# One load of the first image up front, and a last stage without reset, in a selective scan followed by a spiking neuron

## What is computed

```python
x = x + ss2d(group_norm(x))                 # x: 8 images of 48 x 48 x 256, f32
x = x + lif(group_norm(x) @ W.T + b)        # one "time step" is one image

def ss2d(x):        # D = 512 channels, 16 states, L = 2304 positions
    xh, z = split(x @ W_in)
    xc = depthwise_conv_3x3(xh)
    dt, B, C = ...                          # from xc @ W_xproj; dt by softplus
    h = exp(dt * A) * h + (dtN * B) * xc    # scan over L, for each of 16 states
    y = sum(h * C) + Dskip * xc
    return (layer_norm(y) * silu(z)) @ W_out + b_out

def lif(h):         # over the images, one after the other; v = membrane
    v = v + (h_t - v) / 2
    s = (v >= 1)
    v = v * (1 - s)                         # the reset: used by the next image only
    return s                                # spikes
```

## Time and profile before

| | us |
|---|---|
| median of 3 runs | 4572.82 |
| lowest, highest | 4570.01, 4573.57 |
| profiled execution | 4570.02 |
| its span, first to last instruction | 4568.0 |
| TensorE, matmul busy | 3595.8 (79%) |
| VectorE busy | 4081.0 (89%) |
| ScalarE busy | 3338.8 (73%) |
| GpSimd busy | 4007.6 (88%) |

### The profile page before, as it was taken

How to read it: one execution, slowest core, us unless ns; L and a number is a source line. 1 busy time by engine, 2 the same in 40 slices (tenths; PEclk the granted TensorE clock), 3 DMA queues, 4 the chain that set the end, 5 groups by cost and what they waited for, 6 DMA issues and landing times.

```text
span 4568.0 us, 74518 instructions
## 1 busy us (share of the span) xinstructions
PE 3595.8 (79%) x20244; PEld 2243.1 (49%) x20244; DVE 4081.0 (89%) x4077; ACT 3338.8 (73%) x5698; POOL 4007.6 (88%) x2661
## 2 busy tenths in 40 slices
PE   4778888878887887878888787877887887788865
PEld 2444544545454554545554454445544554455543
DVE  0999999999999999998999999999999999999993
ACT  2777777777777777777777777777777777777772
POOL 1999999889998899988999889988999889999991
PEclk9899999999999989998999989999899999999977
DMA  3322322332233223322232223222322232223200
GB/s 76 114 66 85 101 61 72 106 88 72 66 100 96 77 59 99 90 77 73 79 102 70 77 71 100 80 73 73 106 83 63 78 108 88 59 82 95 79 29 21
DMA packets 189416, 364.40 MB, mean 80 GB/s; under 512 B 27416, under 2 KB 164120, under 8 KB 188960
## 3 DMA queue, kind: packets, MB, share of 16 engines
q1 hardware_dynamic: 188960, 359.12, 26.7%
HBM read 289.84 MB, written 69.21 MB: 79 GB/s over the span
## 4 chain that ended last, share of the span: by engine, by line
POOL 33%; issue 26%; PE 16%; DVE 16%; ACT 7%; DVEq 1%; POOLq 1%; DMA 1%; SPq 0%; ACTq 0%
POOL st L562 27%; DVE st L1003 11%; PE ht L1126 6%; DVE y L979 2%; PE work L1192 2%; POOL y L595 2%; PE work L1158 2%; ACT decay L704 2%; PE work L1163 1%; PE work L1153 1%; POOL xb L604 1%; POOL st L569 1%; PE work L1199 1%; DVE work L944 1%; PE work L1099 1%
## 5 line engine op out<-in xcount | busy, mean ns | idle before, releaser
L1003 DVE TENSOR_TENSOR_SCAN st<-decay,st 128x1024 f32<-128x1024 f32 (+1 forms) x1536 | 2732.4, 1779 | 167.6 <-ACT decay L704 75.1
L562 POOL TENSOR_TENSOR st<-xc,bbc 128x1536 f32<-128x1536 f32 x768 | 2652.2, 3454 | 25.1 <-DMA bbc<-brow 12.1
L704 ACT ACTIVATE decay<-dt,neg_a 128x1024 f32<-128x1024 f32 (+1 forms) x1536 | 1361.8, 900 | 513.8 <-DVE st L1003 510.9
L1126 PE MATMUL ht<-ident,st 128*128 128x128 f32 x9216 | 1372.4, 300 | 448.4 <-DVE st L1003 370.7
L1126 PEld LDWEIGHTS ht<-ident,st 128*128 128x128 f32 x9216 | 1145.5, 154 | 775.5 <-issue 439.7
L979 DVE SCALAR_TENSOR_TENSOR y<-ht,ct,y 128x512 f32<-128x512 f32 x1536 | 1121.6, 730 | 94.7 <-PE ht L1126 94.4
L595 POOL TENSOR_TENSOR y<-y,weighed 128x512 f32<-128x512 f32 x624 | 793.1, 1271 | 208.9 <-ACT weighed L733 206.3
L733 ACT ACTIVATE weighed<-ht,ct 128x512 f32<-128x512 f32 x624 | 426.6, 684 | 291.0 <-PE ht L1126 289.3
L1158 PE MATMUL work<-xn,win 128*128 128x384 f32 x768 | 340.9, 588 | 133.2 <-DVE volt L959 100.7
L1099 PE MATMUL work<-tri,conv_w 96*32 96x384 f32 x4608 | 430.0, 507 | 19.0 <-ACT xc L689 13.1
L1153 PE MATMUL work<-xn,win 128*128 128x480 f32 x768 | 356.4, 588 | 5.1 <-ACT xn L836 3.1
(11 more groups left out here) (100 smaller groups left out, 3535.9 us busy)
## 6 DMA issues: line engine op xcount, KB each, us to landing
bbc<-brow SPq DMA_DIRECT2D x192, 768.0 KB, 6.1
tri<-rows_of_xh SPq DMA_DIRECT2D x576, 200.0 KB, 3.9
rows_of_xh<-xhp SPq DMA_DIRECT2D x192, 250.0 KB, 2.6
xin<-in_x_dram SPq DMA_DIRECT2D x48, 384.0 KB, 3.3
out_dram<-ot SPq DMA_DIRECT2D x48, 384.0 KB, 4.1
brow<-xp SPq DMA_DIRECT2D x48, 24.0 KB, 1.5
win<-in_L_conv_W_in_dram SPq DMA_DIRECT2D x1, 1024.0 KB
wo<-in_L_conv_W_out_dram SPq DMA_DIRECT2D x1, 512.0 KB
```

What stands on the lines that cost most here:

```text
L562: u = g.tensor_tensor(slot, xc[:, kq % 2, :, :], bbc[:, piece_slot(kq, p), n % PIECE, :].unsqueeze(1).to_broadcast([P, DC, T]), ALU.mult)
L704: a.activation(flat(decay[:, :, :])[:, lo:hi], flat(dt[:, (k + ahead) % 2, :, :])[:, lo:hi], ACT.Exp, scale=neg_a[:, n:n + 1]).then_inc(s_ ...
L1003: v.tensor_tensor_scan(state[:, lo:hi], flat(decay[:, :, :])[:, lo:hi], state[:, lo:hi], 0.0 if h == 0 else state[:, lo - 1:lo], ALU.mult, ...
L1126: last = t.transpose(ht[:, m, c * P:(c + 1) * P], st[:, j, c, m * P:(m + 1) * P], ident[:, :])
```

## The change

At the start, all six tiles of the first image's x are loaded by six DMAs, ahead of all weights, into the buffer `st`, which the scan doesn't use until the first scan input. TensorE begins with the transposes of x, once GpSimd's constants are there and all six loads have landed; W1's transposes, ScalarE's `neg_a`, VectorE's `w1t` and `neg_a`, and GpSimd's `skip_diag` and `conv_w` stand at the beginning of chunk 5 of image -1, behind the first two projections. The first projection waits for the weights and for the cleared `xhp`, the convolution for the weights' constants. GpSimd clears `xhp` and `volt` behind the identity and the group matrix.

At the end, `walk` stops after chunk 1 of image B. The last image's neuron is written out behind it: products into the three `ht` banks in turn, charge in place, fire into one of four slots of `xb`, transposes into the two `work` banks, evictions to six different places (four in `y`, then `ot` and `xin`), and six stores. ScalarE's copy of the membrane and the reset are left out there.

```diff
 def does(b, k):
     if 1 <= b <= B:
-        kinds |= {L1, GN1}
+        kinds.add(GN1)
+    if 1 <= b < B:
+        kinds.add(L1)
...
             for k in range(K):
                 iteration(B - 1, k)
-            for k in range(L1_AT[K - 1] + 1):
+            for k in range(2):
                 iteration(B, k)
+        def first_x(kc):
+            return st[:, :, :, :].rearrange("p j c t -> p (j c t)")[:, kc * NT * C:(kc + 1) * NT * C].rearrange(
+                "p (m c) -> p m c", c=C)
...
             sp.sem_inc(s_out, 16)
-            load_x(-1, 0, 1)
+            for kc in range(K):
+                sp.dma_start(first_x(kc), x_v[0, kc].rearrange("(m p) c -> p m c", p=P)).then_inc(s_xin, 16)
             load(win[:, :, :], w_in.rearrange("(h p) n -> p h n", p=P))
...
             walk(sp, iteration)
+            for kc in range(K):
+                sp.wait_ge(s_end_o, 2 * kc + 2)
+                sp.dma_start(out_v[B - 1, kc].rearrange("(m p) c -> p m c", p=P), end_tile(kc)).then_inc(s_out, 16)
...
 (GpSimd, ScalarE, VectorE: the constants from the weights)
+                if is_first(b) and k == K - 1:
+                    build_weights()
...
 (TensorE)
-            pe.wait_ge(s_w1, 16)
-            pe.wait_ge(s_set_pool, 2)
-            (W1's four transposes)
-            pe.wait_ge(s_set_dve, 2)
-            pe.wait_ge(s_set_pool, 4)
+            pe.wait_ge(s_set_pool, 3)
...
+                if is_first(b) and k == K - 1:
+                    turn_w1()
...
+                            if is_first(b) and c == 0 and k < K - 1:
+                                pe.wait_ge(s_w, N_W)
+                                pe.wait_ge(s_set_pool, 4)
...
-                            pe.wait_ge(s_xin, ((b + 1) * K + kc + 1) * 16)
+                            pe.wait_ge(s_xin, K * 16 if is_first(b) else ((b + 1) * K + kc + 1) * 16)
...
 (VectorE, behind the walk)
+            await_emptied(dve, B, 1, "b1")
+            for j in range(K * CH):
+                kc, h = divmod(j, CH)
+                cols = slice(kc * T, (kc + 1) * T)
+                now = ht[:, j % NHT, 0:T]
+                dve.wait_ge(s_end_l, j + 1)
+                v.scalar_tensor_tensor(out=now, in0=now, scalar=b1s[:, h:h + 1], in1=volt[:, h, cols],
+                                       op0=ALU.add, op1=ALU.add).then_inc(s_end_v, 1)
+                need(dve, s_end_t, 2 * (kc - 1))
+                dve.wait_ge(s_end_v, j + 1)
+                v.scalar_tensor_tensor(out=end_spikes(kc, h), in0=now, scalar=units[:, 1:2],
+                                       in1=img[:, img_par(B, -1), h, cols], op0=ALU.is_ge,
+                                       op1=ALU.add).then_inc(s_end_f, 1)
...
 (TensorE, behind the walk)
+            def end_l1(j):
+                kc, h = divmod(j, CH)
+                need(pe, s_end_f, j - NHT + 1)
+                for hi in range(CH):
+                    last = t.matmul(ht[:, j % NHT, 0:T], w1s[:, hi, h * P:(h + 1) * P],
+                                    img[:, img_par(B, -1), hi, kc * T:(kc + 1) * T],
+                                    start=hi == 0, stop=hi == CH - 1)
+                last.then_inc(s_end_l, 1)
+            def end_turn(kc):
+                pe.wait_ge(s_end_f, CH * (kc + 1))
+                (six transposes of the spikes into work, s_end_t; ScalarE evicts, s_end_o)
...
+            for i in range(NWORK):
+                pe.wait_ge(emptied[i], 1 + max(n for bank, n in TURNS.values() if bank == i))
+            for kc in range(K):
+                end_l1(CH * kc)
+                end_l1(CH * kc + 1)
+                if kc > 0:
+                    end_turn(kc - 1)
+            end_turn(K - 1)
```

More of the change, by code:

```diff
@@ L117, in does, with is_first @@
     return kinds
+def is_first(b):
+    return isinstance(b, int) and b == -1
 def following(b, k):
@@ L465, in iteration @@
                         store(b, kc)
-                if TIN in do and k in TIN_CHUNKS:
+                if TIN in do and not is_first(b) and k in TIN_CHUNKS:
                     load_x(b, TIN_CHUNKS[k][1], 1)
@@ L515, in _, with build_weights @@
                             channel_multiplier=-1).then_inc(s_set_pool, 1)
[L516 to L524, removed]
+            g.memset(xhp[:, :, :, :], 0.0).then_inc(s_set_pool, 1)
+            g.memset(volt[:, :, :], 0.0)
+            def build_weights():
+                pool.wait_ge(s_w, N_W)
+                pool.wait_ge(s_set_pool, 3)
+                for c in range(DC):
+                    g.tensor_scalar(skip_diag[:, c, :], ident[:, :], skip[:, c:c + 1], None, ALU.mult)
+                pool.wait_ge(s_set_dve, 1)
+                g.tensor_tensor(conv_w[:, :, :, :].rearrange("p g t j -> p (g t) j"),
+                                unit[:, :].unsqueeze(1).to_broadcast([TAPS * Q, DC * NQ * TAPS, Q]),
+                                taps[:, :, :].rearrange("p g t -> p (g t)").unsqueeze(2)
+                                .to_broadcast([TAPS * Q, DC * NQ * TAPS, Q]), ALU.mult).then_inc(s_set_pool, 1)
             def scale_input(w, e, b, k):
@@ L839, in normalise_input @@
                     last.then_inc(s_xn, 1)
+                if is_first(b) and k == K - 1:
+                    act.wait_ge(s_w, N_W)
+                    a.activation(neg_a[:, :], a_raw[:, :], ACT.Exp).then_inc(s_set_act, 1)
                 for s in range(NS):
@@ L893, in _ @@
             walk(act, iteration)
+            act.wait_ge(s_yz, B * K * DC)
+            act.wait_ge(s_out, (B - 1) * K * 16 + 16)
+            for kc in range(K):
+                for half, (lo, n) in enumerate(((0, 2), (2, 1))):
+                    act.wait_ge(s_end_t, 2 * kc + half + 1)
+                    a.activation(end_tile(kc)[:, lo:lo + n, :],
+                                 work[:, half, 0:n * C].rearrange("p (m c) -> p m c", m=n),
+                                 ACT.Copy).then_inc(s_end_o, 1)
         @block.vector
@@ L898, in _ @@
             v = nc.vector
-            dve.wait_ge(s_w, N_W)
             dve.wait_ge(s_set_pool, 3)
@@ L1202, in iteration @@
                             kc, h = int(name[2]), int(name[4])
-                            pe.wait_ge(s_xin, ((b + 1) * K + kc + 1) * 16)
+                            tile = first_x(kc) if is_first(b) else xin[:, :, :]
+                            pe.wait_ge(s_xin, K * 16 if is_first(b) else ((b + 1) * K + kc + 1) * 16)
                             for m in range(NT):
-                                last = t.transpose(work[:, i, m * P:(m + 1) * P], xin[:, m, h * P:(h + 1) * P],
+                                last = t.transpose(work[:, i, m * P:(m + 1) * P], tile[:, m, h * P:(h + 1) * P],
                                                    ident[:, :])
```

57 lines of the change are left out of this document (43 added, 14 removed).

## The result

| | before | changed |
|---|---|---|
| median | 4571.41 us (4 runs, 4559.8 to 4573.6) | 4506.85 us (4 runs, 4505.0 to 4507.6) |
| ratio | | 0.986, interval 0.9849 to 0.9872 |
| profiled execution, span | 4568.0 | 4503.0 |

The change makes the kernel 1.4% faster; 4503 had been predicted. The page of the changed kernel (busy time of the engines, chain that ended last by engine) is the old one less its ends: GpSimd and VectorE have the same busy time, and their shares grow because the span is shorter.

The account below looks back on a forecast made before the run. The scan and its input on VectorE and GpSimd bound the body, while latency at the ends is exposed. 4570.0 - 31.9 (head) - 37.9 (tail) = 4500.2; the median, 2.8 us above the profiled run, gives 4503, range 4496 to 4515.

Parts of the forecast that it names:

- Bound and place: Scan and its input on VectorE and GpSimd bound the body, left alone; any gain comes from the two ends.
- Step 1: Head: six back-to-back loads at 387 GB/s bring all of x by 9.2 us, at 253 GB/s by 11.8.
- Step 2: Head: TensorE transposes six tiles back to back at 1.51 us each; the projection could start at 25.3 us.
- Step 3: Head: weights' semaphore at 22.2, 24.8 or 27.5 us gates the first projection; start taken as 25.4, gain 32.4.
- weights late: Head: weights' semaphore comes at 27.5 to 30 us, 2 to 5 us lost, total 4505 to 4508; chance 0.09.
- Step 4: Behind the first projections: moved constants stay hidden, W1's transposes delay the third projection 0.5 us; head gain 31.9 us.
- high, 4498: Head: dense transposes leave the clock up, three projections save 1.67 us each, total 4498; chance 0.07.
- Steps 5 to 7: Tail: no copy or reset, three banks, TensorE the bound at 3.6 us a tile; gain 37.9 us.
- Low clock in the tail: Tail: clock stays at 0.50 or keeps falling back, gain 20.6 instead of 37.9 us, total 4520; chance 0.13.
- Slower: Body: a lower granted TensorE clock eats the 69.8 us from 0.84 downward, total 4597 at 0.82; chance 0.02.
- bounds of 28 to 37: Head: limits of its gain in us; 28 with loads at 253 GB/s, weights at 27.5 and a full microsecond for W1.
- signs of being right: Head: first x transposes at 9 to 10 us, projection 25 to 26, scan input near 83; tail: 28 us after b1s.

Follow-up runs that it names:

- tile semaphores: Against the changed kernel: one semaphore for each of the six first x loads, so TensorE starts a tile when it lands; 4498.9 us (1 run).
- the second profile: The changed kernel run again with no edit, to see how its head varies; 4502.4 us median (4 runs).

## Why the prediction was right, point by point

- **Bound and place.** Right: the body kept its time (4386.3, then 4385.2 and 4382.8), and all but 1.2 us of the gain came from the ends, which add up when taken one by one.
- **Step 1, the loads: the term that was mis-sized most.** All of x at 9.2 us (bound 11.8) was predicted; its first transposes started at 12.31, and in the other profiles with this wait between 10.7 and 12.3. The step divided x's bytes by the rate of a full queue (and its terms, 8.5 + 0.5, give 9.0 and not 9.2). It left out that the weights are issued behind x and had moved 0.8 MB before x was signalled, and the slices at 213 and 251 GB/s. The Trainium skill (DMA: Bandwidth & Descriptors, Anatomy of one DMA) gives its 2.0 us and 436 GB/s in that section for transfers that GpSimd issues, while these are SyncE's; the estimate of 8.3 by it is further off still.
- **Step 2, the pace.** 1.51 us a tile was predicted, 1.80 came: in each pair it is 1.50, but between the pairs TensorE waits 0.58 us for ACT's copy, since the last half tile of a pair and the first of the next have the same bank in the order that is counted out. Twice this is 1.2 us. The prediction assumed that the banks alternate throughout.
- **Step 3, the gate: hidden, but by luck.** The last weight was issued at 25.17 and landed, by an estimate, some 2.6 us later (25.62 to 28.23 with the tile semaphores), so at 27.8, ahead of 29.54. Of the bounds 22.2, 24.8 and 27.5 only the last is near it: the nine tap loads alone kept SyncE from 4.8 to 17.1 us, where before they took 7.0. The gate stayed hidden only because x was late too. In the profiles whose rows show it the last weight landed between 26.1 and 28.3, so had x come at 9.2, the projection would have waited for the weights and not started at 25.4, which is the rival "weights late"; the tile semaphores, where TensorE has x early, show just that.
- **Step 4, what was moved.** conv_w hidden, as said. W1's transposes cost 0.5 us by prediction and nothing by the trace: the third projection comes 8.43 us behind the first in both kernels. What had been taken as fixed was the rest of the way: 57.3 before, and now 60.6 in one profile and 57.7 in the other. The clock, named as a rival in one direction only (high, 4498), went the other way in the profiled execution: the last two convolutions, xp and dn took 3.3 us more than before, which is the whole growth of W. Over all kernels the way lies between 53.6 and 61.0.
- **Steps 5 to 7, the tail.** 28.7 us from b1s predicted, 27.7 measured. The four first products took 8.41 against 8.2. A tile's round is 3.24 and not 3.60 us: a turn takes 0.82 us in the rows, but it starts at 4487.14, before the products ahead of it end at 4487.30, and the next product starts at 4487.79, before the turn ends, so that it adds only 0.49. That TensorE is the bound and VectorE waits was right.
- **The rivals.** Low clock in the tail: not seen in any run with the new tail; it takes 27.1 to 27.7 us in all of them without fillers. The kernel of which the Trainium skill tells (TensorE: Matmul & The Clock Gate, A second HAM failure mode: psum-queue depth-cycling) oscillates for its micro-idles; this stage cycles through three banks without such gaps, and its granted clock stayed at 1.00 from 4482 to TensorE's last transpose. Weights late: not the bound in the changed kernel, though they landed at the edge of that rival's stretch (step 3). Slower: the body did not move that far.
- **The sum.** The head gave 6.9 us less than said (25.0 for 31.9), the tail 1.0 and the body 1.2 more; the profiled execution was 4504.98 where 4500.2 had been worked out, and the median 3.9 us above 4503. The head's 25.0 lie outside the bounds of 28 to 37 that were set for it (the second profile has 29.3), and of the signs of being right the times of the head (9 to 10, 25 to 26, near 83) all came late. The mechanism held; that the total is so close owes something to the tail and the body, which gave back 2.2 us.

## What to carry to other kernels

An engine's queue is a list of gates: at the start of a kernel ask, for each wait, whether what stands behind it needs that data, and give the data that the first work needs a semaphore of its own. When a stage runs alone at the end, drop what only a next round would use, and take the banks that the other work has left free: each helps alone (18.2 and 29.1 us here), both together less than their sum, up to the next engine's bound. When loads share a queue, a full-queue rate is for all that is in it, not for those that you wait for.

## What the runs showed that was not expected

- VectorE's three 32x32 copies of `unit`, 0.71 us in the earlier trace rows, took 5.53 us in every kernel with the new head, from 3.14 to 8.67, while GpSimd cleared xhp and volt (3.04 to 8.27); one of the three took 5.16 of it. Nothing waited for them here. The Trainium skill (SBUF — State Buffer, Who interferes with whom) says that VectorE, in some forms of a copy, and GpSimd share a port pair that one of them holds for a whole instruction; the trace agrees with a copy that gets through only when both clearings, of 1.35 and 3.94 us, are over. It wasn't tested by moving the clearing.
- In one execution TensorE had a granted clock of 0.26, later 0.36, over nearly all of the 9718 us, three to four tenths of what all others had (0.91 to 0.92). The same kernel ran in 4507.5 us later. What caused it is open.
- W, with the clock's rise and fall in it, differs by 2.9 us between two profiles of the changed kernel and by 7.4 over all, and the body differs by 14 us. The late edits are worth 3 us (the tail) and 5 to 9 us (the first projection), no more than that, so their pieces show them and the totals don't.
